# Graph layer on one core: when POOL may gather again into a slot of rows

## The reference, cut to what matters

```python
h = jnp.maximum(_layernorm(x, axis=-1), 0.0)           # x: 3125 x 128
hW = jnp.einsum('nd,tdf->tnf', h, W_edge) + b_edge[:, None, :]   # 16 edge types
msg = hW[etypes, src]                                   # 50000 edges, sorted by dst
seg = dst * T + etypes
counts = segment_sum(ones, seg)
msg = msg / counts[seg][:, None]
agg = segment_sum(msg, dst)
hN = jnp.einsum('nd,tdf->tnf', h, W_node) + b_node[:, None, :]   # 8 node types
x = x + relu(hN[ntypes, arange(N)] + agg)
```

## Time and profile before

| | before |
|---|---|
| median of 3 runs, us | 834.61 (832.97 to 834.98) |
| span of the profiled execution, us | 833.5 |
| PE products, busy us (share) | 413.8 (50%) |
| DVE | 354.8 (43%) |
| ACT | 176.1 (21%) |
| POOL | 386.9 (46%) |
| gathers of the loop (L377) | 360, mean 1007 ns busy, 367.4 us idle before them |

### The profile page before, as it was taken

The page is one execution under the profiler, slowest core; times in us unless marked ns, Lnnn a source line. Parts: engine busy times, 40 slices in busy tenths (PEclk is TensorE's granted clock), DMA queues, the critical chain, the costliest instruction groups (busy, mean ns, idle before and its releaser), DMA issues.

```text
span 833.5 us, 10463 instructions
## 1 busy us (share of the span) xinstructions
PE 413.8 (50%) x3143; PEld 335.0 (40%) x3143; DVE 354.8 (43%) x914; ACT 176.1 (21%) x431; POOL 386.9 (46%) x384
## 2 busy tenths in 40 slices
PE   1210194790690590590580580670670770760898
PEld 1200092580570470470460460560550550650687
DVE  6700066771460460460460560550550640650694
ACT  4500024220220220220220220220220220220350
POOL 6477405347257157157157157067067077076100
PEclk9555556795695695695695795795795785895899
DMA  4622101522222122122122122122132132132120
GB/s 111 183 52 53 35 0 40 192 77 59 73 83 60 67 83 60 67 85 58 65 85 60 63 88 60 60 91 59 57 94 59 58 94 57 57 97 58 62 105 11
DMA packets 32466, 59.95 MB, mean 72 GB/s; under 512 B 7416, under 2 KB 22836, under 8 KB 29236
## 3 DMA queue, kind: packets, MB, share of 16 engines
q1 hardware_dynamic: 19372, 34.83, 12.5%
q0 software_dynamic: 11776, 24.14, 10.8%
q10 hardware_dynamic: 1296, 0.71, 0.4%
HBM read 56.01 MB, written 3.65 MB: 72 GB/s over the span
## 4 chain that ended last, share of the span: by engine, by line
another core or an unknown queue 46%; PE 34%; DVE 7%; issue 6%; ACT 3%; DMA 1%; DVEq 1%; SPq 0%; ACTq 0%
PE acc L698 10%; PE out_ps L338 8%; PE misc L277 5%; PE out_ps L329 4%; PE acc L680 4%; DVE union_a L354 2%; ACT dg L297 2%; PE node_ps L318 1%; DVE S L978 1%; DMA xs<-in_x_dram 1%; DVE oh L969 1%; PE out_ps L331 1%; ACT union_a L535 1%; PE misc L338 0%
## 5 line engine op out<-in xcount | busy, mean ns | idle before, releaser
L377 POOL DMA_INDIRECT G<-h_table,src_s x360 | 362.6, 1007 | 367.4 <-PE acc L698 261.1
L698 PE MATMUL acc<-oh,G 128*128 128x384 f16 (+1 forms) x784 | 140.4, 316 | 304.2 <-ACT G L284 179.8
L978 DVE TENSOR_TENSOR S<-S,acc 128x384 f32 x196 | 107.9, 550 | 378.9 <-remote 256.8
L698 PEld LDWEIGHTS acc<-oh,G 128*128 128x128 f16 x784 | 77.6, 104 | 353.6 <-issue 171.3
L284 ACT ACTIVATE G<-misc 128x256 f16<-128x256 f32 x24 | 9.2, 383 | 457.3 <-remote 378.9
L969 DVE TENSOR_SCALAR oh<-iota,seg_s 128x224 f16<-128x224 f16 (+1 forms) x390 | 98.4, 296 | 1.3 <-issue 1.3
L338 PE MATMUL out_ps<-w_all,union_a 128*128 128x128 f32 x768 | 96.5, 280 | 4.1 <-DVE union_a L354 4.1
L338 PEld LDWEIGHTS out_ps<-w_all,union_a 128*128 128x128 f32 x768 | 91.4, 195 | 5.7 <-DVE union_a L354 5.6
L277 PE MATMUL misc<-hh,union_c 128*128 128x256 f16 x600 | 80.4, 275 | 4.8 <-issue 4.6
L680 PE MATMUL acc<-union_c 128*16 128x44 f16 x392 | 34.7, 255 | 62.4 <-issue 41.6
L277 PEld LDWEIGHTS misc<-hh,union_c 128*128 128x128 f16 x600 | 58.5, 98 | 12.3 <-issue 6.5
(11 more groups left out here) (103 smaller groups left out, 185.7 us busy)
## 6 DMA issues: line engine op xcount, KB each, us to landing
union_b<-rc_table SPq DMA_DIRECT2D x25, 1024.0 KB
G<-h_table,src_s POOLq DMA_INDIRECT x360
h_table<-hh SPq DMA_DIRECT2D x5, 320.0 KB, 2.5
src_row<-in_src_dram SPq DMA_DIRECT2D x24, 64.0 KB
out_dram<-os SPq DMA_DIRECT2D x24, 64.0 KB
xs<-in_x_dram SPq DMA_DIRECT2D x4, 320.0 KB, 5.0
w_all<-in_L_gnn_W_node_dram SPq DMA_DIRECT2D x1, 512.0 KB
xs<-in_x_dram SPq DMA_DIRECT2D x1, 256.0 KB
```

Source lines behind the costliest of these rows:

```text
L377: nc.gpsimd.indirect_dma_start(out=G[:, slot, :], out_offset=None, in_=h_table[:, :], in_offset=bass.IndirectOffsetOnAxis(ap=index, axis=0 ...
L698: last = nc.tensor.matmul(window[:, :, 0:w], G[:, 2 * g_slot + a, part * D:(part + 1) * D], oh[:, o, a, 0:R * w].rearrange("p (t n) -> p t ...
L978: nc.vector.tensor_tensor(span, span, acc[bank][:, 0:R * W].rearrange("p (t n) -> p t n", n=W), ALU.add).then_inc(s_add, 1)
```

## The change

POOL's loop over iterations becomes a function. For iteration 0 it is written out, without the waits at the groups' starts (the waits for the staged halves stay). For iterations 1 to 5 the wait at a group's start is for DVE's additions, in place of PE's sums, and so is the wait ahead of the last pair's gathers.

```diff
-                with pool.Fori(0, ITERS) as i:
+                def body(i, first):
                     for u in range(BODY):
-                        if u % PPB == 0:
-
-                            pool.wait_ge(pair_mm, LATE + BODY * i + u + PPB)
+                        if u % PPB == 0 and not first:
+
+                            pool.wait_ge(s_add, LATE + PER * (i - 1) + u + PPB)
                         if u % (BODY // 2) == 0:
                             pool.wait_ge(staged, 2 * i + u // (BODY // 2) + 1)
                         if u % PPB == 0:
                             may_issue()
                         for a in range(1 if u % PPB == PPB - 1 else 2):
                             gather(pool, 2 * u + a, src_s[:, 2 * u + a:2 * u + a + 1], gathered[u])
-                pool.wait_ge(pair_mm, LATE + BODY * ITERS + PPB)
+                body(0, True)
+                with pool.Fori(1, ITERS) as i:
+                    body(i, False)
+                pool.wait_ge(s_add, LATE + PER * (ITERS - 1) + PPB)
```

## The result

| | before | changed |
|---|---|---|
| median, us | 833.79 (4 runs, 832.68 to 834.98) | 848.67 (4 runs, 847.44 to 849.78) |
| ratio | | 1.0179, 95% interval 1.0156 to 1.0202 |
| span of the profiled execution, us | 833.5 | 845.6 |

The profiled execution of the changed kernel has 847.44 us in all, 1.8 over its span.

A forecast was written before the change was run, and what follows sets the result against it. It took POOL and PE to work in turns, PE's results coming late until shortly after each gather burst. 18.75 - 1.5 - 5.3 - 2 = +10 us gave a predicted median of 844.6 us, range 836 to 851.

The forecast's parts named there:

- (a): POOL's waits in iterations 1 to 5, moved from PE's sums to DVE's adds: hidden by the staging, 0 us.
- (b): First iteration without waits: 15 gathers move from 132.38 to right behind the first burst's 94.54; sum +10 us, once.
- release "4.66 us after that": First burst: PE is released 4.66 us after the last gather, at 117.9 in place of 99.2, costing +18.75 us.
- credit of 1.5: First burst: PE isn't quite still and part of its slow restart may be over by the release; 1.5 us off.
- The stop by the second burst: Group 0's fetch products: with the burst at 132.38 gone, ACT reads PE's last result at once, -5.3 us.
- The clock after that stop: Next group of eight pairs: without the stop PE's clock need not fall to 1.2 GHz, -2 us.
- (c): First iteration written out makes POOL's program about twice as long; read in while POOL is idle or ahead, 0 us.
- Rival 1: First burst: PE's stop has another cause than the gathers and ends at 99.2 regardless; 826.9 us, chance 0.06.
- Rival 3: First burst: a larger credit, from 9 us on, leaves the sum within the noise, +2.5 us; chance 0.07.
- Rival 4: Ten full bursts: the same hold, now on DVE, ends each up to 2 us later, 865 us; chance 0.03.
- Rival 2: POOL's waits on PE's semaphore themselves hold PE; without them PE runs beside POOL, about 560 us; chance 0.04.

The follow-up runs named there:

- E9: Kernel before with only the waits of iterations 1 to 5 moved to DVE's adds, iteration 0's fourth group still waiting; 839.11 against 839.23 us, with PE held.
- E2: Kernel before with only the waits of iterations 1 to 5 moved to DVE's adds; 559.63 against 559.76 us, PE not held.
- E7: E2 run again: kernel before with only the later waits moved to DVE's adds; ratio 0.9994 (559.35 against 559.61 us), PE not held.
- E12: Kernel before, POOL also waiting after each pair's gathers until those of the pair two before have landed; 841.51 against 838.36 us, with PE held.
- E11: Kernel before with ACT staging indices by the group of 8 pairs in place of a half; 748.82 against 840.25 us, with PE held.
- E5: The changed kernel run again beside the kernel before; 853.42 against 840.30 us, with PE held.
- E10: Kernel before without the second gather of each pair, 8 gathers a group in place of 15; 610.73 against 832.43 us, with PE held.
- E1: Kernel before with only iteration 0 written out without waits, later waits still on PE's sums; 559.31 against 559.76 us, PE not held.
- E6: E1 run again: kernel before with only iteration 0 written out without waits; 559.83 against 559.61 us, PE not held.
- E4: Kernel before without the second gather of each pair, 8 gathers a group in place of 15; 429.79 against 559.76 us, PE not held.
- E8: Kernel before with ACT staging indices by the group of 8 pairs in place of a half; 561.19 against 559.61 us, PE not held.

## Why the prediction was right, and where not

- (a), the moved wait, at 0: right. E9 has 0.9998 with the hold, E2 and E7 have 1.0006 and 0.9994 without it.
- (b), the 15 gathers behind the first burst: the last one stands at 113.83, 113.3 forecast. The step that failed is the release "4.66 us after that" with its credit of 1.5. It read DVE's row at 99.20 as the end of the hold. But PE goes on slowly while held, so such a row tells when a given batch has come through. In four traces with the same 51 gathers, the last one at 94.47 to 94.88, that row stands at 95.28 (E9), 99.20 (before), 101.75 (E12) and 103.02 (E11); with 66 gathers it came within the burst, at 92.88 (changed) and 108.56 (E5), and the next one at 124.50, 10.7 us after the last gather. What follows the last gather is the full pace, and the later the longer the burst was: 7.2 us behind it after 30 gathers (E10), 8.7, 8.7, 8.3 and 10.0 after 51 (before, E9, E12, E11), 10.4 and 11.2 after 66 (changed, E5). So the count came 20.8 us late, not 17.25, and the credit has the other sign, +2.0 in place of -1.5: 19.3 us are the gathers themselves, and the full pace comes 1.7 us later behind the last of them. Why it comes later after a longer burst isn't shown.
- The stop by the second burst: -5.3 forecast; measured 20.77 - (174.10 - 157.83) = 4.5 (5.5 between E9 and E5).
- The clock after that stop: -2 forecast, 16.09 - 13.65 = 2.4 measured, with 1.00 granted in 174.70 to 180.20 against 0.53 in the earlier trace rows. E9 took 15.07 us for this group and E5 13.65, so there it was 1.4.
- The sum: 20.8 - 4.5 - 2.4 = 13.9, the +14.0 of the first full burst; between E9 and E5 that burst stands 189.87 - 175.62 = 14.3 us later. The timed runs agree: 14.9 and 13.1. The +10 forecast is 4 us short of that, nearly all of it by the release, and the +14 lies at the upper end of the prediction's own range.
- That the first two spans differ by only 12.1 us is scatter of single profiles. The distance from the first full burst to the next is 58.2 us in the changed kernel's profile and 60.5 in the one before, but 62.3 in E5, 61.5 in E9 and 62.0 in E12, and PE's granted clock is 1.00 at the start of that burst in both (176.20 to 190.00, 190.20 to 204.00). The timed runs differ by 2.8 us more than the profiled ones: every execution listed takes 1.75 to 1.95 us more than its span, so the profiled one before, with 833.5, took an estimated 835.3 us, above all four listed, while the changed kernel's was its quickest (846.7 to 848.0 are the spans of the others).
- (c), the longer program of POOL, at 0: no run has it by itself, but E1 and E6 contain it and show 0.9989 and 1.0012, without the hold.

Rival 1 (PE's stop in the first burst has another cause than the gathers and ends at 99.2 whatever POOL does) is wrong by the changed kernel itself, where full pace moved from 103.28 to 124.25, and by E10, where it came at 75.81. Rival 3 needed a credit of 9 us and got none. Rival 4 (the hold passes to DVE) is wrong by E9. Rival 2 (the wait on PE's semaphore holds PE) is wrong as well: the changed kernel and E5 have no wait of POOL on PE's semaphore in the loop, and PE is held as before. Its time, 560 us, is real, but it is the other condition's, in which the kernel before has it too.

The Trainium skill's rule (SBUF — State Buffer, section "SBUF: two separate sides") that a DMA and a compute operation don't slow each other isn't borne out by E10 against its kernel before. It isn't refuted as a rule on SBUF's ports either, since no run shows that the ports are where PE is held, and E1 to E4 and E6 to E8 had no hold from the same gathers.

What stays open: what holds PE, and why only in some sets of runs. Excluded are the clock, the full queue (E12) and POOL's waits on PE (the changed kernel, E5). Whether POOL's making of the descriptors or the transfers do it was not tried. Two more things on record bear on it. The profile's own records differ: E7 without the hold has 7,312 records of semaphore updates made by DMAs and E9, the same kernel, 2,050, though both moved the same 59.96 MB. All traces with this many gathers fall into these two kinds (7,312 to 7,357 without the hold, 2,046 to 2,336 with it), and in a held burst these records grow sparser towards its end. So the path of these updates, or their recording, may have a part in the hold, as its cause or by its effect; every time here is of an execution that was recorded, so no run tells. And the two sets without the hold are those in which three or four versions ran beside the kernel before (E1 to E4, E6 to E8); with one version beside it, it was there each time (the result, E5, E9 to E12). Neither was tried by itself.

## What to carry to other kernels

A wait that looks idle can be spacing two costs: look not only at what the freed instructions wait for, but at what is slow while they run. Here the fourth group wasn't needed before the second half of the iteration, and asking for it earlier only put 19 us of gathers in front of a count on the critical path. When an engine's results come late in each burst of another one's work, the lever is the length and place of the bursts, as the 91 us of E11 show, not the semaphore that starts them. And such a gain counts only where the hold is met: the same edit was worth nothing where the kernel before took 560 us.

## What the runs showed of the hardware that was not expected

- The same program took 559.6 and 832.4 us on one chip (E8 and E10, the kernel before beside each), and 560 to 840 across chips, with each set of runs within 1.6% of itself.
- With the hold, PE's products in the count came at 1.4 to 2.3 us each on average, at either clock level (28 in 54.5 us and, in E5, 28 in 63.5 us with 0.50 granted, in the changed kernel 22 in 31.7 us with 1.00), against 0.08 us free of it. Late in a long burst they start up to 2.80 us apart (99.04 and 101.84 in the changed kernel), and while it clears 0.70 us apart (121.45 to 123.55). PE's records can run far ahead of its results: recorded to 373.4, read at 404.78 in the earlier trace rows. The wait rows then say "remote" or "issue", and the time only shows in the engine that reads the result.
